# Layer 1 expert weights: GpSimd subtracts every low part straight into its slot, with no transfer inside SBUF

## The reference, cut to what matters

```
xf = layernorm(x)                                   # 1024 x 384
shared = (silu(xf @ Wg_s) * (xf @ Wu_s)) @ Wd_s     # 384 -> 768 -> 384
logits = xf @ W_router + expert_bias                # 8 experts
top_vals, top_idx = top_k(logits, 2);  rw = softmax(top_vals)
routed = sum over the 2 chosen e of  rw * ((silu(xf @ Wg_r[e]) * (xf @ Wu_r[e])) @ Wd_r[e])
x = x + shared + routed
```

## Time and profile before

| | us |
|---|---|
| median of 3 runs | 1055.59 |
| lowest and highest | 1055.34, 1055.71 |
| the profiled execution, its own time | 1051.15 |
| its span, first to last instruction | 1049.4 |

### The profile page before, as it was taken

The page is one execution under the profiler, slowest core; times in us unless marked ns, Lnnn a source line. Parts: engine busy times, 40 slices in busy tenths (PEclk is TensorE's granted clock), DMA queues, the critical chain, the costliest instruction groups (busy, mean ns, idle before and its releaser), DMA issues.

```text
span 1049.4 us, 14337 instructions
## 1 busy us (share of the span) xinstructions
PE 973.8 (93%) x4756; PEld 641.0 (61%) x4757; DVE 544.5 (52%) x960; ACT 322.8 (31%) x482; POOL 519.5 (50%) x375
## 2 busy tenths in 40 slices
PE   6999999999998999998598989699899999999998
PEld 3755555555546566665456555368666677677764
DVE  4466888888665355554555675871122222222224
ACT  2524455655721122221325555051111111111100
POOL 5614778898821122220634766646667667700014
PEclk9999999999998999999899999889999999999999
DMA  9679708000056357311435200504777777731015
GB/s 318 161 190 336 168 1 181 21 1 1 1 192 243 130 189 242 144 61 36 128 98 126 62 1 8 218 1 169 259 255 256 255 260 265 255 123 42 16 51 152
DMA packets 52493, 147.43 MB, mean 140 GB/s; under 512 B 7153, under 2 KB 26105, under 8 KB 52184
## 3 DMA queue, kind: packets, MB, share of 16 engines
q1 hardware_dynamic: 37080, 80.00, 25.1%
q0 software_dynamic: 15360, 66.73, 18.6%
HBM read 87.78 MB, written 29.03 MB: 111 GB/s over the span
## 4 chain that ended last, share of the span: by engine, by line
PE 66%; POOL 13%; DVE 8%; DMA 7%; issue 4%; ACT 3%; DVEq 0%; SPq 0%; POOLq 0%; ACTq 0%
PE PS L2111 15%; PE PS L2133 8%; POOL raw L1026 6%; PE PS L1838 6%; PE PS L1874 6%; PE PS L1737 5%; PE PS L1894 5%; DMA raw<-in_Wg_r 5%; PE PS L1876 5%; PE PS L2016 3%; PE PS L2159 3%; POOL Wgu L1024 2%; DVE nmax L1426 2%; PE PS L1803 2%; PE PS L1748 2%
## 5 line engine op out<-in xcount | busy, mean ns | idle before, releaser
L1224 ACT ACTIVATE expS<-PS 128x1024 f32<-128x1024 f32 (+3 forms) x156 | 135.3, 877 | 106.4 <-PE PS L1876 104.8
L2133 PE MATMUL PS<-Wd,hidT 128*128 x414 | 142.8, 491 | 1.7 <-DVE hidT L1624 1.0
L953 POOL TENSOR_TENSOR exp_acc<-exp_acc,expS 128x512 f32<-128x512 f32 (+1 forms) x65 | 135.2, 2089 | 16.4 <-ACT expS L1224 14.7
L1874 PE MATMUL PS<-QA,KS 128*128 128x512 f32 (+3 forms) x312 | 116.5, 379 | 4.1 <-ACT QB L1202 3.5
L1426 DVE TENSOR_REDUCE nmax_part<-PS 128x1 f32<-128x512 f32 x160 | 105.5, 682 | 27.6 <-PE PS L1838 27.5
L1838 PE MATMUL PS<-KS,QA 128*128 128x512 f32 (+2 forms) x288 | 108.0, 401 | 9.5 <-DVE nmax L1426 5.1
L1876 PE MATMUL PS<-QB,KS 128*128 128x512 f32 (+3 forms) x312 | 109.9, 358 | 0.0
L2133 PEld LDWEIGHTS PS<-Wd,hidT 128*128 128x128 f32 x414 | 78.8, 192 | 48.9 <-issue 4.1
L2111 PE MATMUL PS<-Wgu,xbT_high 128*128 x207 | 91.1, 440 | 10.6 <-DMA Wgu_low<-raw 7.0
L2111 PE MATMUL PS<-Wgu,xbT 128*128 x276 | 97.4, 490 | 1.8 <-ACT xbT L1321 1.7
L1339 ACT ACTIVATE hidT<-PS 128x384 f32<-128x384 f32 x46 | 22.6, 491 | 236.3 <-PE PS L2119 236.3
(11 more groups left out here) (195 smaller groups left out, 1611.8 us busy)
## 6 DMA issues: line engine op xcount, KB each, us to landing
Wgu_low<-raw POOLq DMA_DIRECT2D x15, 1152.0 KB, 6.0
Wgu<-in_Wgu SPq DMA_DIRECT2D x8, 1152.0 KB, 5.8
raw<-in_Wu_r POOLq DMA_DIRECT2D x8, 1152.0 KB, 7.2
Wd<-in_Wd_r POOLq DMA_DIRECT2D x8, 1152.0 KB, 9.0
raw<-in_Wg_r POOLq DMA_DIRECT2D x7, 1152.0 KB, 8.7
part_rows<-parts SPq DMA_DIRECT2D x2, 3072.0 KB, 17.9
Wd<-in_Wd SPq DMA_DIRECT2D x8, 576.0 KB, 7.7
block_rows_in<-zero_src SPq DMA_DIRECT2D x1, 4416.0 KB, 15.7
```

What stands on the lines that cost most here:

```text
L953: last = pool.tensor_tensor(acc, older, exp_tile(0, c, u)[:, pair, heads], ALU.add)
L1224: act.activation(exp_tile(layer, c, unit)[:, pair, :].rearrange("p (b n) -> p b n", b=2)[:, :, lo:hi], PS[:, 2 * pair:2 * pair + 2, lo:hi] ...
L1874: pe.matmul(PS[:, 2 * pair + j, lo:hi], keys, QA[layer][c % 2][:, g, queries], start=True, stop=False)
L2133: last = pe.matmul(PS[:, 7, 0:C], hidT[layer][:, par, i, :], Wd[layer][:, bass.ds(s, 1), i, :], start=i == 0, stop=i == m.IC - 1)
```

## The change

POOL subtracts every low part from the raw half straight into the expert's low slot, so the copies within SBUF and their semaphores `low_placed` are gone, and PE waits for `low_done` instead. The raw half of expert q+1 is loaded as soon as the low part of expert q is done, part by part. For expert 0 the order is changed: SP loads `raw_first` during the attention (once the scores of the second chunk are done), POOL casts part 0 once the first half of the normalised rows is done, casts part 1 behind the six shared chunks, and subtracts both parts behind the scatter. The high slots move by 18,432 bytes within their region, `gu_hi` and the second low slot too.

```diff
-        Wgu.append(at("Wgu1", [P, 2, 2, KC, 2 * I1], 0, F32R))
+        Wgu.append(at("Wgu1", [P, 2, KC, 2 * I1], 4 * KC * 2 * I1, F32R))
...
-        gu_hi = at("gu_hi", [P, KC, 2 * I1], slot_gu, F32R)
+        gu_hi = at("gu_hi", [P, KC, 2 * I1], 0, F32R)
...
-        low_step = (arena + 4 * KC * 2 * I1 - lane) // 4
+        low_step = (arena - lane) // 4
...
+            sp.wait_ge(score_psum, 2 * (PV_BEFORE[1] + 2 * U[1]))
+            sp.dma_start(raw_first[:, :, :].bitcast(F32), Wg_r[0].rearrange("(k p) n -> p k n", p=P)).then_inc(raw_first_in, 16)
             sp.wait_ge(sums_psum, 2 * BLOCKS)
...
-                def split(q, part):
+                def low_of(q, part):
+                    low = Wgu_low[:, q % 2, 0:KC * 2 * m.I].rearrange("p (k n) -> p k n", k=KC)
+                    return low[:, :, part * m.I:(part + 1) * m.I]
+                def high_part(q, part):
                     own = raw_of(q, part)
-                    pool.wait_ge(raw_in[part], 16 * (q + 1))
+                    if (q, part) == (0, 0):
+                        pool.wait_ge(raw_first_in, 16)
+                    else:
+                        pool.wait_ge(raw_in[part], 16 * (q + part))
                     pool.tensor_copy(high_of(q, part), own[:, :, :].bitcast(F32)).then_inc(high_done, 1)
+                def low_part(q, part):
                     pool.wait_ge(high_done, 2 * q + part + 1)
-                    pool.tensor_tensor(own[:, :, :], own[:, :, :].bitcast(F32), high_of(q, part).bitcast(F32),
-                                       ALU.subtract).then_inc(low_done, 1)
-                def place_low(q, part):
-                    low = Wgu_low[:, q % 2, 0:KC * 2 * m.I].rearrange("p (k n) -> p k n", k=KC)
-                    pool.wait_ge(low_done, 2 * q + part + 1)
-                    pool.dma_start(low[:, :, part * m.I:(part + 1) * m.I].bitcast(F32), raw_of(q, part)[:, :, :].bitcast(F32)).then_inc(low_placed[part], 16)
-                def next_raw(q):
+                    pool.tensor_tensor(low_of(q, part), raw_of(q, part)[:, :, :].bitcast(F32),
+                                       high_of(q, part).bitcast(F32), ALU.subtract).then_inc(low_done, 1)
+                def split_and_load(q):
                     for part in range(2):
-                        pool.wait_ge(low_placed[part], 16 * (q + 1))
+                        high_part(q, part)
+                        low_part(q, part)
                         if q + 1 < E:
+                            pool.wait_ge(low_done, 2 * q + part + 1)
                             load_raw(q + 1, part)
...
                 def shared_low_parts():
                     pool.wait_ge(normalised, normalised_before(2 * BLOCKS - 1) + TAIL_CUTS)
-                    for part in range(2):
-                        load_raw(0, part)
-                    for part in range(2):
-                        split(0, part)
+                    load_raw(0, 1)
+                    pool.wait_ge(xn_ready, 3 * NT + NT // HALF)
+                    high_part(0, 0)
                     for f in range(m.IC):
                         pool.wait_ge(gu_hi_ready, f + 1)
                         pool.tensor_tensor(chunk_of(gu_lo, f), chunk_of(shared_gu, f), chunk_of(gu_hi, f).bitcast(F32),
                                            ALU.subtract).then_inc(gu_lo_ready, 1)
+                    high_part(0, 1)
...
                 def expert_weights():
                     pool.wait_ge(scattered, 16 * TOP * NT)
+                    load_raw(1, 0)
                     for part in range(2):
-                        place_low(0, part)
-                    next_raw(0)
+                        low_part(0, part)
+                    pool.wait_ge(low_done, 2)
+                    load_raw(1, 1)
                     pool.wait_ge(shared_psum, HALF * m.IC)
                     pool.wait_ge(shared_hid, HALF * m.IC)
                     load_down(0, 0)
...
                         if layer:
-                            for part in range(2):
-                                pe.wait_ge(low_placed[part], (q + 1) * 16)
+                            pe.wait_ge(low_done, q * 2 + 2)
```

More of the change, by code:

```diff
@@ L349, in build @@
         scattered = sem("scattered")
-        low_placed = [sem(f"low_placed{n}") for n in range(2)]
         low_done = sem("low_done")
@@ L353, in build @@
         raw_in = [sem(f"raw_in{n}") for n in range(2)]
+        raw_first_in = sem("raw_first_in")
         high_done = sem("high_done")
@@ L1012, in high_of @@
                 def high_of(q, part):
-                    return Wgu[1][:, q % 2, 0, :, part * m.I:(part + 1) * m.I]
+                    return Wgu[1][:, q % 2, :, part * m.I:(part + 1) * m.I]
                 def load_raw(q, part):
@@ L1018, in load_raw @@
                                    (Wg_r, Wu_r)[part][q].rearrange("(k p) n -> p k n", p=P)).then_inc(raw_in[part], 16)
-                def split(q, part):
+                def low_of(q, part):
+                    low = Wgu_low[:, q % 2, 0:KC * 2 * m.I].rearrange("p (k n) -> p k n", k=KC)
+                    return low[:, :, part * m.I:(part + 1) * m.I]
+                def high_part(q, part):
                     own = raw_of(q, part)
-                    pool.wait_ge(raw_in[part], 16 * (q + 1))
+                    if (q, part) == (0, 0):
+                        pool.wait_ge(raw_first_in, 16)
+                    else:
+                        pool.wait_ge(raw_in[part], 16 * (q + part))
                     pool.tensor_copy(high_of(q, part), own[:, :, :].bitcast(F32)).then_inc(high_done, 1)
+                def low_part(q, part):
                     pool.wait_ge(high_done, 2 * q + part + 1)
-                    pool.tensor_tensor(own[:, :, :], own[:, :, :].bitcast(F32), high_of(q, part).bitcast(F32),
-                                       ALU.subtract).then_inc(low_done, 1)
-                def place_low(q, part):
-                    low = Wgu_low[:, q % 2, 0:KC * 2 * m.I].rearrange("p (k n) -> p k n", k=KC)
-                    pool.wait_ge(low_done, 2 * q + part + 1)
-                    pool.dma_start(low[:, :, part * m.I:(part + 1) * m.I].bitcast(F32), raw_of(q, part)[:, :, :].bitcast(F32)).then_inc(low_placed[part], 16)
-                def next_raw(q):
-                    for part in range(2):
-                        pool.wait_ge(low_placed[part], 16 * (q + 1))
-                        if q + 1 < E:
-                            load_raw(q + 1, part)
+                    pool.tensor_tensor(low_of(q, part), raw_of(q, part)[:, :, :].bitcast(F32),
+                                       high_of(q, part).bitcast(F32), ALU.subtract).then_inc(low_done, 1)
                 def split_and_load(q):
                     for part in range(2):
-                        split(q, part)
-                        place_low(q, part)
-                    next_raw(q)
+                        high_part(q, part)
+                        low_part(q, part)
+                        if q + 1 < E:
+                            pool.wait_ge(low_done, 2 * q + part + 1)
+                            load_raw(q + 1, part)
                 def load_down(e, slot):
@@ L2103, in gate_up @@
                         if layer:
-                            high = lambda kc: Wgu[1][:, bass.ds(s, 1), 0, kc, lo:lo + n]
+                            high = lambda kc: Wgu[1][:, bass.ds(s, 1), kc, lo:lo + n]
                             low = lambda kc: Wgu_low[:, bass.ds(s, 1), kc * 2 * m.I + lo:kc * 2 * m.I + lo + n]
```

## The result

The changed kernel takes 1030.36 us (median of four executions, 1025.65 to 1032.09), the kernel before in the same comparison 1055.65 (1055.34 to 1057.32): a ratio of 0.975, interval 0.9713 to 0.9787. The profiled execution took 1028.77 us, its span 1027.0. Forecast were 1033.9 and, for a profiled execution, 1029.5. One later execution of before, 1071.34 us at a mean granted clock of 0.930 where the others have 0.973 to 0.982, is a slow one and is left out of every count.

The account below looks back on a forecast made before the run. Bounds named: PE's four waits (7.0 us) for copied low parts, and DVE stalled by POOL in layer 1's second normalisation. 10.6 + 11.05 = 21.7 us off the median 1055.59 gave 1033.9 us, range 1031 to 1041.

Parts of the forecast that it names:

- Step 1: Second normalisation of layer 1: kept clear of POOL, the logits start at 680.02, not 690.62, 10.6 us earlier.
- most of the rest: Router before the logits: its full clock makes up most of the 10.6 us beyond 8.7 us of DVE stalls.
- Step 2: First expert's low parts, now made after the scatter: done at 732.6, costing nothing on the path to block 0.
- its cover: Ahead of block 0: low parts done 0.8 us before PE wants them, 0.2 us with subtracts at 5.44.
- the two numbers: Routing before the scatter: part 1's cast delays it by 2.1 us, or by nothing if DVE gets in first.
- Rival two: Expert 0's low parts end last: block 0 later by 1 to 2 us, total 1035 to 1038; chance 0.15.
- Step 3: Routed blocks of later experts: all four PE waits for copied low parts go, worth 11.05 us.
- The sum: Whole kernel: 10.6 + 11.05 = 21.7 us, taken from the median of 1055.59 to give 1033.9 us.
- The range: Whole kernel: 1031 to 1041 us; the forecast as worked out, 1031 to 1035, had chance 0.67.
- Rivals one and three: Normalisation stays held up, 1039 to 1044.5 us (chance 0.08); raw loads come too late, 1039.5 to 1045 (0.06).
- rival four: Subtract into a slot costs much more than in place: kernel slower, about 1067 us at 10.3 each; chance 0.03.

## Why the prediction was wrong, and where it was right

**Step 1, right.** ACT's `logits_t` was forecast at 680.02 and came at 679.74. On the first two profiled executions 10.7 us went out of the stretch to the logits, 10.6 were forecast. The first cast had the room that was worked out. What the text called "most of the rest", the router at full clock, is a term of its own: the run with one cast in the normalisation shows 1.8 us of stall and 2.0 us of what follows it on PE, and in the six traces of before the stretch runs from 20.7 to 22.3 us. One reading was too wide: not every DVE instruction from SBUF to SBUF stood still. In the kernel before the statistics at 671.29 took 0.56 us beside POOL's subtract, as they do alone at 671.09 after.

**Step 2, right, and its cover not needed.** The cast did cost the routing 2.0 us (2.18 for an addition of 0.20) and the low parts were done within 0.1 us of the forecast. The Trainium skill (SBUF — State Buffer, section "SBUF: two separate sides") has an exclusive lock on the ports that the two engines share: of GpSimd and a VectorE instruction that uses these ports, whichever starts first has them for a whole instruction. What DVE does in the traces agrees. In the changed kernel the cast started at 691.60 and the addition at 691.61, and the addition ended with the cast. In the run with the cast among the normalisation, DVE's timeline and then POOL's have

```profile
695.72 0.20 DVE L1557 TENSOR_TENSOR tile_cum<-tile_cum 128x56 f32<-128x56 f32 x1
695.96 1.97 DVE L1556 COPY tile_cum<-tile_cum 128x16 f32<-128x16 f32 x1
```

```profile
695.73 2.17 POOL L1034 CAST Wgu<-raw 128x2304 fp32r<-128x2304 f32 x1
```

The addition that started 0.01 us ahead of the cast took 0.20 us; the copy behind it took 1.97, until the cast had ended. Whether POOL waited for that addition in its turn, its 2.17 us do not show. So the choice between the two numbers was a matter of hundredths of a us, and it decided nothing: with the cast out of the way block 0 comes at the same distance from the logits. Rival two came true by the name in the bracket, and cost nothing.

**Step 3, its mechanism right, its size taken from too little.** All four waits went, the subtract kept its 5.1 us, blocks follow 11.05 us apart. Between the first two profiled executions block 0 to block 13 is 11.5 us shorter (153.95 and 142.44), 11.05 forecast. But block 0 ran at the lower clock in both of them, and before that came off the next wait. Between the second traces, where it ran at full clock in both, the blocks as a whole are 266.38 and 253.12 us long: 13.3 us.

**The sum is the step that failed**: "I take the difference from the median". The 21.7 us were the difference of one execution of before, and that was a short one: of the 46 others timed here only six were shorter, and their median is 1054.4. To take them from the median is to hold that the 4.4 us up to it lie in work which both kernels share. By medians they lie in the two places that the change removes: the slots alone are worth 15.0 us where the sum has 11.05, and the new order on top of them 11.5 where it has 10.6, together 26.6 for 21.7.

The traces show how that can be. The term of 7.0 us of waits and 4.1 us of clock behind them is 5.0 us larger in the execution at 1057.25, and the 10.6 us of step 1 are up to 1.5 us larger. Over the six traces the collision is 21.3 us and the blocks 267.2 us in the mean; the changed kernel has 10.07 and, in its two traces, 253.9. That is 11.3 + 13.3 = 24.6 us in the two places; the spans lie 24.1 us apart in the mean, since the changed kernel reached the router 0.5 us later. The medians lie 25.3 us apart in the first comparison and 26.6 in the second. The 1.2 to 2.5 us that are left no trace explains: five of the six traced executions of before took less than 1052.6 us, but only seven of the 41 others, so an execution of median length is not among them, and whether the six are short by chance is not shown.

The range failed with the same step: its low end allowed for a wait less at block 0 and for nothing in the terms themselves, though a cost that hangs on the clock behind a wait was in the sum, read from one trace. Rivals one and three did not happen, as the rows of DVE and POOL show; rival four is excluded by the 5.12 us of the subtract. That the waits and the clock behind them vary from one execution to the next is shown; what decides it in an execution isn't, and was not tried.

## What to carry to other kernels

Before a saving is taken off a median, see where the profiled execution stands among the timed ones; if it is a short one, the missing time can lie, as here by the medians, in the very waits that are to be removed, so their price needs more than one trace. A stall of VectorE beside GpSimd, on a path that feeds TensorE, can cost more than its length, since TensorE may come back from it at the lower clock: 3.75 us for 1.8 in one run here, 10.7 us for 8.7 in the kernel before. And the name in a wait's bracket is that of the end that came last: whether it also cost something is shown by the distance to the other ends.

## What was not expected of the hardware

- The same wait of PE, 1.9 to 2.0 us ahead of block 0, was followed by 0.86 of the clock over 12 us in some executions of either kernel and by 1.00 in others, a difference of 1.6 us.
- 2.28 us of GpSimd among the normalised activations cost 3.75 us at the logits.
- With the copies within SBUF gone (147.43 MB moved before, 128.55 after) the raw loads, as large as they are, land in 5.9 us in the median, where the earlier trace rows have 8.1. The loads also go out at other times than before, and no run separates the two; with the copies put back and the new order kept they took 7.9. The view of that line after:

```profile
DMA to landing us min/median/max: 5.6/5.9/9.2
```
